# Expert slices, combinations and gathers one chunk sooner, and an image's scatter in two chunks instead of three

## What is computed

```python
x = x + conv(_gn(x), L0_conv_weight)              # group norm, 3x3 convolution
t = _to_tokens(x)                                 # (8, 3136, 64)
t = t + attn(_ln_t(t), Wq, bq, Wk, bk, Wv, bv)    # softmax over 3136 keys, per image
t = t + ffn(_ln_t(t), gate_w, gate_b, w1, w2, w3) # 16 experts, each token uses its best 2
x = _from_tokens(t, x)
```

## Time and profile before

| | us |
|---|---|
| median of 3 runs | 2741.71 (2737.01 to 2741.85) |
| profiled execution, span of its instructions | 2736.8 |
| PE busy | 2503.4 (91%) |
| DVE busy | 1832.0 (67%) |
| ACT busy | 1316.8 (48%) |
| POOL busy (without the issue time between DMAs) | 1019.0 (37%) |
| attention bodies 0 to 55 | from 111.0 to about 2500 |

### The profile page before, as it was taken

How to read it: one execution, slowest core, us unless ns; L and a number is a source line. 1 busy time by engine, 2 the same in 40 slices (tenths; PEclk the granted TensorE clock), 3 DMA queues, 4 the chain that set the end, 5 groups by cost and what they waited for, 6 DMA issues and landing times.

```text
span 2736.8 us, 46413 instructions
## 1 busy us (share of the span) xinstructions
PE 2503.4 (91%) x13821; PEld 1603.6 (59%) x13821; DVE 1832.0 (67%) x5227; ACT 1316.8 (48%) x2985; POOL 1019.0 (37%) x1097
## 2 busy tenths in 40 slices
PE   4799999999999999999999999999999999997773
PEld 2455555566666666566666666566666666564662
DVE  3666677676766777676867777676867776764432
ACT  1244444455554555455555555455555555453542
POOL 2012104400344324442344334443344324465765
PEclk8899999999999999999999999999999999998876
DMA  2124211111122122122121212122121111122442
GB/s 61 39 64 90 50 28 40 48 37 39 48 55 61 47 57 62 54 53 55 55 61 52 57 46 70 55 54 52 53 60 51 44 47 53 54 50 64 120 95 53
DMA packets 226555, 152.94 MB, mean 56 GB/s; under 512 B 100240, under 2 KB 216720, under 8 KB 226320
## 3 DMA queue, kind: packets, MB, share of 16 engines
q1 hardware_dynamic: 192208, 98.97, 14.0%
q0 software_dynamic: 31456, 48.03, 7.1%
q10 hardware_dynamic: 2656, 2.98, 0.4%
HBM read 83.92 MB, written 65.27 MB: 55 GB/s over the span
## 4 chain that ended last, share of the span: by engine, by line
PE 62%; DVE 13%; issue 5%; DMA 2%; POOL 2%; SPq 1%; ACT 1%; POOLq 0%; DVEq 0%; ACTq 0%
PE ps_o L1466 16%; PE ps_s L1454 8%; PE ps_m L1426 8%; PE ps_s L1455 7%; PE ps_x L1625 4%; DVE max_part L1105 4%; PE ps_z L1639 3%; PE ps_z L1492 3%; PE ps_x L1632 2%; PE ps_z L1614 2%; PE ps_y L1529 1%; DMA tc<-kept 1%; PE ps_s L1625 1%; PE ps_y L1545 1%; POOL got L783 1%
## 5 line engine op out<-in xcount | busy, mean ns | idle before, releaser
L1105 DVE TENSOR_REDUCE max_part<-ps_m 128x1 f32<-128x448 f32 x1400 | 858.6, 621 | 517.1 <-PE ps_m L1426 497.0
L950 ACT ACTIVATE prob<-ps_s 128x448 f32<-128x448 f32 x1400 | 757.3, 543 | 527.0 <-PE ps_s L1455 502.9
L1466 PE MATMUL ps_o<-prob,v_s 128*64 128x448 f32 x2800 | 683.0, 562 | 0.0
L1454 PE MATMUL ps_s<-q_a,k_a 128*128 128x448 f32 x1400 | 593.5, 424 | 1.6 <-ACT q_a L942 0.7
L783 POOL DMA_INDIRECT got<-sorted_y,slot x448 | 428.3, 956 | 433.0 <-PE ps_s L1455 209.5
L762 POOL DMA_INDIRECT sorted_x<-xn,slot x448 | 429.8, 959 | 350.3 <-issue 154.7
L1426 PE MATMUL ps_m<-k_a,q_a 128*128 128x448 f32 (+3 forms) x1600 | 530.0, 358 | 28.2 <-DVE max_part L1105 22.4
L1455 PE MATMUL ps_s<-q_b,k_a 128*128 128x448 f32 x1400 | 511.9, 366 | 0.0
L1426 PEld LDWEIGHTS ps_m<-k_a,q_a 128*128 128x128 f32 (+1 forms) x1600 | 298.7, 188 | 92.7 <-DVE max_part L1105 61.5
L1454 PEld LDWEIGHTS ps_s<-q_a,k_a 128*128 128x128 f32 x1400 | 265.9, 190 | 142.3 <-ACT prob L950 106.5
L1466 PEld LDWEIGHTS ps_o<-prob,v_s 128*64 128x64 f32 x2800 | 153.5, 135 | 224.9 <-issue 161.1
(11 more groups left out here) (186 smaller groups left out, 3031.6 us busy)
## 6 DMA issues: line engine op xcount, KB each, us to landing
fx<-sorted_x SPq DMA_DIRECT2D x43, 384.0 KB
sorted_y<-fy SPq DMA_DIRECT2D x42, 320.0 KB
xh<-in_x SPq DMA_DIRECT2D x96, 126.0 KB, 2.7
fx<-sorted_x SPq DMA_DIRECT2D x47, 256.0 KB
sorted_x<-fy POOLq DMA_DIRECT2D x28, 320.0 KB, 6.0
sorted_x<-xn,slot POOLq DMA_INDIRECT x448
got<-sorted_y,slot POOLq DMA_INDIRECT x448
x_now<-in_x SPq DMA_DIRECT2D x112, 56.0 KB, 2.3
```

Of the source, the lines that this page charges most:

```text
L950: a.activation(prob[(at.n * KEY_TILES + i) % PROBS][:], ps_s[(at.n * KEY_TILES + i) % 2][:, 0:CHUNK], ACT.Exp).then_inc(s["p_ready"], 1)
L1105: v.tensor_reduce(max_part[n % 2][0:here.stop - here.start, j, kb:kb + 1], ps_m[(passes_before(n) + m) % 2][0:here.stop - here.start, 0:CH ...
L1454: t.matmul(ps_s[t_of % 2][:, 0:CHUNK], k_a[p][:, keys], high, start=True, stop=False)
L1466: t.matmul(ps_o[side:side + CHANNELS, 0:CHUNK], v_s[u % 2][:, i, :], prob[(n * KEY_TILES + i) % PROBS][:], start=(i < 2), stop=(i >= KEY_T ...
```

## The change

Everything that follows the routing of an image is placed one body sooner: the expert slices (`LAG`), the codes, the combinations, the gathers, and the point where the last image's slices begin (`TURN`, from `LAG`) and where the late combinations begin (`LATE`). The scatter then has two bodies. One combination of chunk 6 goes alone to c = 0 of the following image, one of chunk 5 alone to c = 6. New step tables stand for bodies of 12 and of 16 moves; before, such bodies spread their moves evenly (for 16: steps 0, 1, 3, 4, 6, 7, 9, ...).

```diff
-LAG = {"pre": -CHUNKS, "post": 1, "experts": CHUNKS + 4}
-SCATTERED_TO = (0, 0, 9, 19, PER * CHUNKS)
-COMBINES = {4: ((1, 0),), 5: ((0, 1), (1, 2)), 6: ((0, 3), (1, 4)), 8: ((0, 5), (1, 6))}
-COMBINES_LAST = {4: ((1, 0),), 5: ((0, 1), (1, 2)), 6: ((0, 3), (1, 4)), 7: ((0, 5),), 8: ((0, 6),)}
-GATHERS = {4: (0, 1), 5: (2, 3), 6: (4, 5), 7: (6,)}
+LAG = {"pre": -CHUNKS, "post": 1, "experts": CHUNKS + 3}
+SCATTERED_TO = (0, 0, 16, PER * CHUNKS)
+COMBINES = {3: ((1, 0),), 4: ((0, 1), (1, 2)), 5: ((0, 3), (1, 4)), 6: ((0, 5),), 7: ((0, 6),)}
+COMBINES_LAST = COMBINES
+GATHERS = {3: (0, 1), 4: (2, 3), 5: (4, 5), 6: (6,)}
 NORM2_AT, NORM1_AT, RSTD_AT = 7, 11, 14
 MOVES_AT = {4: (13, 16, 19, 22), 8: (1, 4, 8, 12, 15, 17, 19, 21), 9: (1, 4, 8, 11, 13, 15, 17, 19, 21),
-            10: (0, 2, 4, 8, 12, 14, 16, 18, 20, 22)}
+            12: (0, 1, 3, 4, 6, 7, 9, 10, 12, 14, 16, 18), 16: (1, 2, 4, 5, 7, 8, 10, 11, 13, 14, 16, 17, 19, 20, 22, 23)}
-LATE = ALL + 5
+LATE = ALL + 4
-CODES_AT = {CHUNKS * (g + 1) + 3: g for g in range(BATCHES - 1)}
+CODES_AT = {CHUNKS * (g + 1) + 2: g for g in range(BATCHES - 1)}
@@ def moves_at
-        if self.c == 4 and many == 2 * PER:
+        if self.c == 3 and many == 2 * PER:
             return MOVES_AT_STORED
```

## The result

| | before | after |
|---|---|---|
| time, median of 4 runs | 2740.8 us (2737.0 to 2741.9) | 2757.8 us (2752.7 to 2759.9) |
| ratio, with its 95% interval | 1 | 1.0062 [1.0049, 1.0072] |
| span of the profiled execution | 2736.8 us | 2758.1 us |
| attention, first to last score product of L1454 | 2388.8 us | 2425.1 us |
| what lies behind the last score product | 237.0 us | 221.3 us |

The changed kernel is slower by 17 us; 2753 was forecast, with a range from 2736 to 2768. The two spans differ by 21.3 us: the attention is longer by 36.4, the tail shorter by 15.7, and 0.7 lies ahead of the attention. One of the six runs of the kernel of experiment 1 took 3283.2 us at a granted clock of 0.684 and is counted in that kernel's median of 2733.0 us; the other five alone have 2732.5.

The account below looks back on a forecast made before the run. The prediction took TensorE, busy for 2503.4 of 2736.8 us, as the bound. Its terms, -14.2 + 5.3 + 1.8 + 0 + 18.5 = +11.4 us, were added to the median 2741.7 to give 2753, range 2736 to 2768.

Parts of the forecast that it names:

- The tail: After the last attention body: one five-pair slice and chunk 41's combination leave, scatters and late gathers start sooner; -14.2 us.
- One more slice beside attention: Body 10 gets a slice beside its attention and the codes go to body 9; +5.3 us.
- The short slice: The two-pair slice and the code reductions move from c = 3 to c = 2; +1.8 us.
- The combinations: An image's seven combinations move to c = 3, 4, 5, 6, 0 and stay seven; 0 us.
- The scatters: 16 and 12 moves at c = 1 and 2 delay POOL's second-norm power (L801), and TensorE waits; +18.5 us.
- A: Faster: the late second-norm power costs nothing, as TensorE's later waits on VectorE absorb it; 2734.6 us, chance 0.20.
- D: About no change: half of the second-norm power's lateness is absorbed; 2744 us, chance 0.13.
- C: Scatters aren't through at the end of c = 2 and the slices wait; 2760 us, chance 0.05.
- B: Much slower: TensorE stands over 6 us in body 9 and its clock falls, also body 51; 2767 us, chance 0.12.

Follow-up runs that it names:

- experiment 1: Changed kernel with two to four of a body's twelve scatter moves ahead of the second norm's power (L801) instead of five: 2733.0 us, ratio 0.9970.
- held kernel: The kernel of experiment 1: the changed kernel with some scatter moves held back until the second norm's power is out; 2733.0 us.
- Experiment 5: Load of `tc` issued ahead of the `x_st` loads: kernel before 2731.0 us, held kernel 2722.9; issued a body earlier, ahead of the `fy` store: 2727.3 and 2713.8.
- experiment 2: Changed kernel with six scatter moves instead of five ahead of the second norm's power in bodies of 12 moves: 2782.8 us, ratio 1.0166.
- experiment 3: Kernel before with only the scatter changed, to 16 and 12 moves at c = 1 and 2: 2773.3 us, ratio 1.0115.

## Why the prediction was right in kind and too low in size

**The tail, -14.2: right.** The tail shrank by 15.7 us, and slice 49 starts 15.0 sooner behind the last body. The last scatter starts 55.2 us behind the last body where it was 64.9, 9.7 sooner for the 12 forecast, and the first late gather 13.5 sooner for 14.6. Both chains moved together, as the step said; the gather follows the last scatter directly now and waits for no store.

**One more slice beside attention, +5.3: right.** The bodies 9 and 10 of the held kernel sum to 83.5 us, for 78.9: +4.6.

**The short slice, +1.8: slightly high.** The five bodies at c = 2 without lateness (16 to 44) last 42.1 us on average (42.0 said), those at c = 3 43.6 (43.8 said). The five pairs cost 0.7 us together, and the bodies 51 and 52 nothing.

**The combinations, 0: right as a sum, by luck in its parts.** The remainder of the held kernel's attention against before is -0.3 us. But it is made of larger parts, among them +2.7, +1.9, +1.7 and +1.5 in the bodies 26, 53, 49 and 34, and -1.9, -1.6 and -1.5 in the bodies 50, 20 and 29. The step named the cause (the load of `tc` behind the store and two loads) and then costed it as the same in each body. Experiment 5 measures it: 13.6 us in the kernel before and 18.6 in the held one.

**The scatters, +18.5: the mechanism right, the lateness slightly high, its price too low.** The steps on POOL's line held: L797 at 25.5 us into body 15 for 25.6 said; L801 in body 9 at 22.7 for 23.0, in the bodies at c = 2 at 18.2 to 18.8 for 19.0, in body 51 at 17.5 for 18.2. With 1.3 us more in body 55 than before, lateness sums to 15.1 us where 18.5 was forecast, and the wait for L801 grew by 15.7. Most of the 3.4 us too much is a slip in the working. From L797 at 25.6, its 1.04 and 18 DMAs at 1.247 POOL is through at 49.1 us after the body's start, not at 49.9, and L801 at c = 2 starts at 18.2, which is what the trace shows. So the power is 0.7 us late there and not 1.5, in five bodies.

Then the prediction took one microsecond of time for one of wait. That is the term that was too small. Medians give 25.5 us for the 17.1 us of wait between the held and the changed kernel. The two errors partly cancel: with 15.1 for 18.5 the same sum would have given 2750. That 2753 came as near to 2757.8 as it did is luck in this part. The two profiled executions differ more, by 31.4 in the attention; the changed one is the slowest of its four runs, and the held one the fastest of its six.

The mean granted clocks, changed kernel first, then held:

```profile
core 0: 2758.1 us, clock 0.955
...
core 0: 2727.8 us, clock 0.965
```

0.010 of 2758 us, divided by the half that the lower level takes off, are some 55 us more at that level. The kernel before has 0.965 too. TensorE's busy time of 17.2 us over before fits this, since the products are the same.

**Rivals.** A (2734.6, chance 0.20) and D (2744, chance 0.13) fall by experiments 1 and 2: nothing of a wait is taken back. A's figure is what the kernel costs when the power isn't late at all, 2733.0. C isn't seen: the slices don't wait for the last scatter. B (2767, chance 0.12) was right in its mechanism and too narrow in where it applies. It let the clock fall in the bodies 9 and 51, where TensorE stands for 8.0 and 4.4 us, and there it fell. But it falls in body 16 behind 1.9 us too, and below 1.00 in 13 of the bodies from 9 to 55; two of them (54 and 55) are so in the kernel before, and three (26, 34 and 55) in the held one. What kept the time under B's figure is that the lateness at c = 2 was 0.7 to 1.3 us and not 2.5. The forecast and B were one mechanism: a lateness and its clock belong in one term.

Two of the prediction's readings of the kernel before don't hold. It gives body 55 a clock of 0.96 "where the power was late". But the lower level begins at 2467.5 there, ten us ahead of L801 (2477.52), behind a stop of 2.47 us that a combination made:

```profile
2467.72 0.98 PE L1553 MATMUL ps_y<-ident,t_out 112*128 112x112 f32 x4 [2.47 <-DVE t_out L1296]
```

And VectorE is not busier in body 55 than in the tail: 13.64 of 38.6 us, against 12.95 of 30.0 from 2535 to 2565. Nor are there many copies in a body; body 16 has three, of 0.2 to 0.3 us each. So these rows couldn't tell whether VectorE stretches the issues. Body 9 of the changed kernel is the better row: VectorE is busy for 29 of 47 us there and the DMAs start 1.24 us apart, though it has hardly a copy either.

The Trainium skill (TensorE: Matmul & The Clock Gate, HAM oscillation) says that gaps in TensorE's work bring the clock down again and again. The trace agrees in kind, with 0.51 behind a stop of 1.9 us in body 16 and 0.96 over body 26, where the stop was 2.0. These stops are shorter than those of the section's example, and not each of them does it: see below. The prediction cited that rule for B alone and left its price out of its own sum; with 2 to 4 us on top, as worked out there, it would have been 2755 to 2757, and with the lateness as it was, 2752 to 2754.

**Where the 17 us stand.** In the profiled executions: -15.7 tail, +4.6 slice, +0.7 short slice, -0.3 combinations, +31.4 between the held and the changed kernel, +0.7 ahead of the attention: 21.4 for a difference of the spans of 21.3. Of the 31.4, 26.9 stand in the eight bodies of the table and 4.4 in the bodies 40, 49 and 54, where no power is late. There TensorE stands 1.5, 1.1 and 1.8 us for L1105 behind the combination at step 0, which waits for `tc` (4.69, 2.07 and 2.65 us), and a few us at the lower level follow. In the held kernel the stops at the same places are 1.1, 1.1 and 2.4 us, and the clock stays at 1.00. So these 4.4 us belong to experiment 5 and to this one execution, not to the power.

**What stays open.** Why the same lateness of 0.7 us leaves the clock low for some 7 us in the bodies 16 and 37 and for half of that in body 23. The stops before it are 1.9 us each. More widely, when a stop of 2 us brings the clock down: those of 2.0 us ahead of L1538 in body 10 of the kernel before and in body 9 of the held one, and of 2.4 us in body 54 of the held one, left it at 1.00. So the price of 1.4 to 1.7 us for a us of wait is a mean over many stops of this kernel and not that of a single one.

## What to carry to other kernels

When a queue of indirect DMAs is packed into fewer stages, count how many of its issues stand ahead of each small operation that the same engine owes to the critical path; the issues cost time there, wherever their data goes. Issues held back until that operation was out were worth 25.5 us here, and a load issued ahead of a store that waits was worth 13.6 to 18.6. And where TensorE is the bound, price a stop of one or two microseconds above its length: 1.4 to 1.7 times it on average here.

## What the runs showed of the hardware that was not expected

- TensorE's granted clock goes to 0.51 for 7 us of full work behind a stop of only 1.9 us (body 16). A power that was late by 0.7 us was enough for it: body 16 lasts 42.0 us held and 44.9 late. A stop of 2.07 us in body 10 of the kernel before was not enough; that body is at clock 1.00.
- The slope of time against wait was about the same over two steps, 25.5 us for 17.1 and 27.4 for 19.9, and somewhat steeper in experiment 3, 31.8 for 19.0.
- POOL's issue rate of indirect DMAs didn't move: 0.94 us and 0.30 between them, in the body 9 of the changed kernel beside a VectorE busy for 29 of 47 us, as in the tail. One more move ahead of L801 shifted it by 2.5 us in each of eight bodies.
- A load issued 1.9 us after a body's store and behind two others kept VectorE standing 5.15 us (issue 1211.31, reader 1215.00); issued 7.3 us ahead of the body's start it was no wait at all.
